# Two buffers for the raw attention outputs, one PSUM bank for the value products, three for the maximum scores

## The reference

```
xn = layernorm(x)
q, k, v = heads of (xn Wq^T / 4), (ctx Wk^T), (ctx Wv^T)
scores[q,k] = q.k + (q . p_params)[clip(q-k, -4, 4) + 4], -1e30 where k > q
x = x + tanh(g_xattn) * (softmax(scores) v, heads joined) Wo^T
```

## Time and profile before

| | us |
|---|---|
| median of 3 runs (lowest, highest) | 740.97 (736.86, 741.93) |
| the profiled execution: its time | 738.62 |
| its span | 736.7 |
| prologue, to the first score of unit 0 | 0 to 65.1 |
| units 0 to 5, start of each | 65.1, 103.2, 145.1, 185.5, 225.1, 265.6 |
| units 6 and 7, start of each | 306.0, 340.3 |
| end of the last value product of unit 7 | 369.7 |

### The profile page before, as it was taken

One profiled execution on the slowest core, in us unless ns is written; L12 is line 12 of the kernel. 1 busy time (PEld: TensorE's weight loads), 2 busy tenths in 40 slices (PEclk: granted clock), 3 DMA queues, 4 the chain that ended last, 5 costly groups with the idle time before them and its releaser, 6 DMA issues.

```text
span 736.7 us, 10646 instructions
## 1 busy us (share of the span) xinstructions
PE 628.5 (85%) x3384; PEld 484.8 (66%) x3384; DVE 460.5 (63%) x884; ACT 277.4 (38%) x501; POOL 176.7 (24%) x177
## 2 busy tenths in 40 slices
PE   3674968788878977888647999999999999999997
PEld 2553745457545754554325888888888888888886
DVE  3567657777578758762168475755747575665653
ACT  2432456244643465335333333323232333324222
POOL 2142004310341007100010223232323223232322
PEclk9756989899989999989868999999999999999999
DMA  7741133513344333454121103121211202121220
GB/s 234 210 103 36 30 86 85 114 41 86 72 107 97 73 78 95 99 168 127 40 48 60 57 7 98 41 87 57 81 63 53 91 1 100 43 86 58 74 72 28
DMA packets 39856, 58.65 MB, mean 80 GB/s; under 512 B 7984, under 2 KB 21040, under 8 KB 39792
## 3 DMA queue, kind: packets, MB, share of 16 engines
q1 hardware_dynamic: 39824, 58.25, 28.9%
HBM read 31.76 MB, written 4.85 MB: 50 GB/s over the span
## 4 chain that ended last, share of the span: by engine, by line
issue 49%; PE 20%; DVE 10%; POOL 8%; DMA 6%; SPq 3%; ACT 2%; POOLq 0%; DVEq 0%; ACTq 0%
POOL hl L1150 4%; PE oT L915 4%; PE smax L854 4%; SPq L277 2%; DMA qs<-mt 2%; DVE mx L582 2%; PE oT L919 2%; PE sT L895 2%; DMA at<-rden_d 2%; PE work L794 2%; PE sT L894 2%; DVE mx L609 1%; DMA rden_d<-dent 1%; POOL d L380 1%; PE work L825 1%
## 5 line engine op out<-in xcount | busy, mean ns | idle before, releaser
L1150 POOL TENSOR_TENSOR hl<-sg,hh 128x512 fp32r<-128x512 f32 x72 | 93.0, 1293 | 249.3 <-ACT hh L1193 249.3
L482 ACT ACTIVATE ex<-sT 128x512 f32<-128x512 f32 (+1 forms) x160 | 92.2, 590 | 152.1 <-PE sT L895 127.6
L1187 ACT ACTIVATE sg<-pg 128x512 f32<-128x512 f32 x72 | 43.0, 597 | 198.8 <-PE pu L1432 198.0
L854 PE MATMUL smax<-km,qs 96*128 96x308 f32 (+1 forms) x240 | 91.2, 412 | 27.1 <-DVE mx L582 19.3
L582 DVE TENSOR_REDUCE mx<-smax 128x2 f32<-128x308 f32 x184 | 82.9, 474 | 48.3 <-PE smax L854 45.4
L854 PEld LDWEIGHTS smax<-km,qs 96*128 96x128 f32 x240 | 47.8, 206 | 72.8 <-DVE mx L582 40.1
L1447 PE MATMUL py<-wxl,hh 128*128 128x256 f32 x288 | 81.8, 284 | 3.1 <-DVE x L1331 2.0
L1447 PE MATMUL py<-wxh,hl 128*128 128x256 f32 x288 | 80.9, 281 | 0.0
L1447 PE MATMUL py<-wxh,hh 128*128 128x256 f32 x288 | 80.6, 280 | 0.0
L1319 DVE TENSOR_TENSOR sg<-cwb,sg 128x512 f32<-128x512 f32 x64 | 67.2, 1050 | 11.3 <-DMA cwb<-cwt_d 8.4
L1314 DVE TENSOR_TENSOR sg<-pu,sg 128x512 f32<-128x512 f32 x72 | 49.2, 683 | 28.0 <-ACT sg L1187 26.6
(11 more groups left out here) (152 smaller groups left out, 1124.1 us busy)
## 6 DMA issues: line engine op xcount, KB each, us to landing
cwb<-cwt_d SPq DMA_DIRECT2D x64, 256.0 KB, 3.4
qs<-qh SPq DMA_DIRECT2D x64, 128.0 KB, 2.6
qs<-ql SPq DMA_DIRECT2D x32, 128.0 KB, 2.8
at<-rden_d SPq DMA_DIRECT2D x64, 64.0 KB, 2.2
out<-x SPq DMA_DIRECT2D x8, 512.0 KB, 4.4
ks<-km SPq DMA_DIRECT2D x16, 231.0 KB, 3.4
wx<-in_wx SPq DMA_DIRECT2D x9, 384.0 KB, 6.6
x<-in_x SPq DMA_DIRECT2D x3, 1024.0 KB, 8.8
```

What stands on the lines that cost most here:

```text
L482: nc.scalar.activation(ex[:, g % 2, i % 5, q0:HALF], ST[i % 2][:, q0:HALF], ACT.Exp).then_inc(exp_s, 1)
L854: last_one = nc.tensor.matmul(bank[:, k, 0:width], qs[0:96, s, tile * P:(tile + 1) * P], km[:, s, 0:width], start=True, stop=True)
L1150: nc.gpsimd.tensor_tensor(hl[:, i % R, :], sg[:, i % R, :], hh[:, i % R, :], ALU.subtract).then_inc(hl_done, 1)
L1187: nc.scalar.activation(sg[:, i % R, :], PG[i % RG][:], ACT.Silu).then_inc(sg_s, 1)
```

## The change

- `raws` is a pair: a new SBUF buffer `raw_first` for units with h=0 and the old `raw` for h=1. `raw_out` of unit u waits only for the division of unit u-2. `divisors` and `divide` take the buffer of their unit.
- `OT` is one bank. A value product of group g waits until the copy of the group before it is done. The copies move to after exponentials 9, 14, 19, and 4 of the next unit.
- `SM` has three banks, and block q = 2p + k uses bank q mod 3, so it waits for the reader of block q-3, where it was q-2. In the prologue the ring has five banks (three of `SM`, two of sT) in place of two pairs.

```diff
+    raw_first = sb("raw_first", [P, NG, HALF])
+    raws = (raw_first, raw)
...
-    SM = ctx.enter_context(nc.psum_tensor("smax", [P, 2, HALF], F32))
+    SM = ctx.enter_context(nc.psum_tensor("smax", [P, 3, HALF], F32))
...
-    M_START = (SM, STP)
-    OT = [ctx.enter_context(nc.psum_tensor(f"oT{i}", [P, HALF], F32)) for i in range(2)]
+    MAX_BANKS = [SM[:, i, :] for i in range(3)]
+    M_START = MAX_BANKS + ST
+    OT = ctx.enter_context(nc.psum_tensor("oT", [P, HALF], F32))
...
+    RING = 3
+    def is_near(h, q):
+        return h == 0 and m_tile(0, q // 2) < 2
+    def copied(q):
+        return sum(is_near(0, i) for i in range(q))
+    def reduced(h, q):
+        return sum(not is_near(h, i) for i in range(q))
...
-        def raw_out(u, g, start=False):
+        def raw_out(u, h, g):
             act.wait_ge(pv_ps, NG * u + g + 1)
-            if not start:
-                act.wait_ge(at_s, 2 * (u - 1) + g % 2 + 1)
-            nc.scalar.copy(raw[:, g, :], OT[g % 2][:]).then_inc(raw_s, 1)
+            if not (isinstance(u, int) and u < 2):
+                act.wait_ge(at_s, 2 * (u - 1))
+            nc.scalar.copy(raws[h][:, g, :], OT[:]).then_inc(raw_s, 1)
...
-                if i == 5 and carry:
-                    raw_out(u - 1, 3, start=(h == 1 and isinstance(b, int) and b == 0))
+                if i == 4 and carry:
+                    raw_out(u - 1, 1 - h, 3)
...
-                if i in (14, 17, 19):
-                    raw_out(u, (14, 17, 19).index(i), start=not carry)
+                if i in (9, 14, 19):
+                    raw_out(u, h, i // 5 - 1)
...
-                nc.vector.tensor_tensor(at[:, g, :], raw[:, g, :], at[:, g, :], ALU.mult).then_inc(at_s, 1)
+                nc.vector.tensor_tensor(at[:, g, :], raws[h][:, g, :], at[:, g, :], ALU.mult).then_inc(at_s, 1)
...
+            q = 2 * p + k
+            if q == 0:
+                pe.wait_ge(mx_s, 3 * NM * b + NM * h)
+            elif q >= RING and is_near(h, q - RING):
+                pe.wait_ge(sx_s, NM * b + copied(q - RING + 1))
+            elif q >= RING:
+                pe.wait_ge(mx_s, 3 * NM * b + NM * h + reduced(h, q - RING + 1))
+            stack_scores(m_tile(h, p), p, k, MAX_BANKS[q % RING])
...
-                if not (start and g < 2):
-                    pe.wait_ge(raw_s, NG * u + g - 1)
+                if not (start and g == 0):
+                    pe.wait_ge(raw_s, NG * u + g)
...
-                    nc.tensor.matmul(OT[g % 2][32 * j:32 * j + 32, :], va[:, 4 * g + j, :], ex[:, g % 2, j, :],
+                    nc.tensor.matmul(OT[32 * j:32 * j + 32, :], va[:, 4 * g + j, :], ex[:, g % 2, j, :],
```

More of the change, by code:

```diff
@@ L262, in m_stack, with divisors @@
                          mt[:, q0:HALF].unsqueeze(1).broadcast_to([32, NSTK, HALF - q0]).bitcast(F32)).then_inc(ms_in, 16)
-        def divisors(u):
+        def divisors(u, h):
+            kept = raws[h]
             sp.wait_ge(raw_s, NG * (u + 1))
-            sp.dma_start(den_d.rearrange("j (g n) -> j g n", g=NG), raw[HD::32, :, :]).then_inc(den_out, 16)
+            sp.dma_start(den_d.rearrange("j (g n) -> j g n", g=NG), kept[HD::32, :, :]).then_inc(den_out, 16)
             sp.wait_ge(den_out, 16 * (u + 1))
@@ L290, in unit @@
             if carry:
-                divisors(u - 1)
+                divisors(u - 1, 1 - h)
             if h == 1 and ahead:
@@ L324, in sync @@
         batches(sp, unit)
-        divisors(2 * B - 1)
+        divisors(2 * B - 1, 1)
     def gpsimd(pool):
@@ L460, in q_out, with near @@
                 nc.scalar.copy(qh[:, c, :], W[(use + c) % 2][:]).then_inc(q_hi, 1)
-        def near(b, p, bank=SM):
+        def near(b, p, banks=MAX_BANKS):
             for k in range(2):
-                act.wait_ge(sm_ps, 4 * NM * b + 2 * p + k + 1)
-                nc.scalar.copy(sx[:, m_tile(0, p), m_stacks(p).start + k, :], bank[:, k, 0:SW]).then_inc(sx_s, 1)
-        def raw_out(u, g, start=False):
+                q = 2 * p + k
+                act.wait_ge(sm_ps, 4 * NM * b + q + 1)
+                nc.scalar.copy(sx[:, m_tile(0, p), m_stacks(p).start + k, :], banks[q % len(banks)][:, 0:SW])\
+                    .then_inc(sx_s, 1)
+        def raw_out(u, h, g):
             act.wait_ge(pv_ps, NG * u + g + 1)
-            if not start:
-                act.wait_ge(at_s, 2 * (u - 1) + g % 2 + 1)
-            nc.scalar.copy(raw[:, g, :], OT[g % 2][:]).then_inc(raw_s, 1)
+            if not (isinstance(u, int) and u < 2):
+                act.wait_ge(at_s, 2 * (u - 1))
+            nc.scalar.copy(raws[h][:, g, :], OT[:]).then_inc(raw_s, 1)
         def unit(b, h, carry, ahead):
@@ L576, in k_lo, with maximum @@
                                                ALU.mult, ALU.subtract).then_inc(kl_s, 1)
-        def maximum(b, h, p, bank=SM):
+        def maximum(b, h, p, banks=MAX_BANKS):
             for k in range(2):
+                q = 2 * p + k
                 stk = m_stacks(p).start + k
-                dve.wait_ge(sm_ps, 2 * NM * (2 * b + h) + 2 * p + k + 1)
+                dve.wait_ge(sm_ps, 2 * NM * (2 * b + h) + q + 1)
                 nc.vector.reduce_max(mx[:, m_tile(h, p), 2 * stk:2 * stk + 2],
-                                     bank[:, k, 0:PAIR].rearrange("p (j k) -> p j k", j=2), AX_X).then_inc(mx_s, 1)
+                                     banks[q % len(banks)][:, 0:PAIR].rearrange("p (j k) -> p j k", j=2), AX_X)\
+                    .then_inc(mx_s, 1)
         def by_stack(ap):
@@ L642, in reciprocals, with divide @@
             nc.vector.reciprocal(dent[:], dent[:]).then_inc(rden_s, 1)
-        def divide(u, groups=range(2)):
+        def divide(u, h, groups=range(2)):
             dve.wait_ge(rden_in, 128 * (u + 1))
@@ L740, in vector @@
             if m_tile(0, p) >= 2:
-                maximum(0, 0, p, M_START[p % 2])
+                maximum(0, 0, p, M_START)
             if p == 8:
@@ L757, in last_residual @@
                 residual(B - 1, 1, pr, NW0 + Y_USE[0] + pr)
-        return lambda: reciprocals(2 * B - 1), lambda: divide(2 * B - 1), last_residual
+        return lambda: reciprocals(2 * B - 1), lambda: divide(2 * B - 1, 1), last_residual
     def tensor(pe):
@@ L978, in tensor @@
             for k in range(2):
[L980 to L988, removed]
+                q = 2 * p + k
+                last = q - len(M_START)
+                if last >= 0 and is_near(0, last):
+                    pe.wait_ge(sx_s, copied(last + 1))
+                elif last >= 0:
+                    pe.wait_ge(mx_s, reduced(0, last + 1))
+                stack_scores(m_tile(0, p), p, k, M_START[q % len(M_START)])
         max_T(0, 0, -1, START + 12)
```

28 lines of the change are left out of this document (8 added, 20 removed).

## The result

The changed kernel took 729.42 us (median of 4 runs, 728.44 to 732.39) beside 741.45 for the kernel before (4 runs, 736.86 to 742.01), a ratio of 0.9844 with a 95% interval of 0.9811 to 0.9876. It is 1.6% faster, 12.0 us by the medians, where 727 was forecast; the time stands inside the range of 719 to 735. The profiled execution took 729.36 us with a span of 727.3, against 738.62 and 736.7 before.

A forecast was written before the change was run, and what follows sets the result against it. PE carries most work, so its idle places at waits for maxima and a raw copy count. 5.3 + 7.2 + 0.4 + 0.5 = 13.4 us off 738.62 gives 725.2, or 727.6 from the median: forecast 727, range 719 to 735.

The forecast's parts named there:

- (a): Units 1, 3 and 5, step 16: the ring moves work into PE's pause, 2.4 us three times, 7.2 in all.
- Rival B: The clock is not lowered after the shorter pause at step 16, 3 x 2 us more: 721 us, chance 0.11.
- DVE behind POOL: Units 1, 3 and 5: two divisions still take 4.4 us beside POOL's 3.61 us subtraction; the pause can only be filled.
- The single bank: Value products: one bank costs nothing, as the copy ends 1.5 us early; 0.1 to 0.3 us a group in units 6, 7.
- Rival D: The copy is late at the single bank, 31 products lose 0.6 us each, 18.6 in all: 746 us, chance 0.06.
- (b): Unit 7: PE's 6.03 us wait for the raw copy goes and the projection starts 5.3 us earlier, a gain that stays.
- (c): Unit 6, step 15: one block moves ahead of PE's 2.52 us pause for maxima, 0.4 us gained.
- The prologue: Before unit 0: with five banks the fifth block no longer waits 0.77 us for a copy; 0.5 us, bounds 0 and 0.8.
- Units 2 and 4: PE's early pause there: no gain counted, since the transposes behind it need DVE's normalised rows, which come at the same time.
- (2): Units 1, 3, 5: value matmuls before a 2.5 to 2.9 us pause ending at DVE's maximum, clock about 0.5, 2.4 us shorter each.
- Rival C: The step 16 pause is not filled because the value product is held there; only 5.3 + 0.4 + 0.5 remain: 735, chance 0.09.
- E: Rival: unit 7 gives nothing because its end is held by its own division's DMA chain: 733 us, chance 0.08.

The follow-up runs named there:

- e2: The changed kernel with the ring of maximum scores back at two banks, four in the prologue: 737.75 us, ratio 0.9953 to the kernel before.
- e5: The changed kernel with the odd units' value product of step 16 put behind the second block of maximum scores: 735.92 us, ratio 0.9931 to the kernel before.
- e6: The changed kernel with POOL's subtraction done for half of the stacks only, so less work and different output: 720.25 us, ratio 0.9745 to the kernel before.
- e4: The changed kernel with DVE's divisions in the odd units moved behind the maxima of step 17: 724.16 us, ratio 0.9783 to the kernel before.
- e1: The kernel before with the second raw buffer alone, keeping its ring of two and two product banks: 739.16 us, ratio 0.9986.
- e9: The changed kernel with the odd units' divisions behind step 17 and two maximum banks again in even units: 723.07 us, ratio 0.9762 to the kernel before.
- e3: The changed kernel with four banks in the prologue instead of five, the ring of three kept inside the units: 731.37 us, ratio 0.9875 to the kernel before.
- b2: The kernel before, unchanged, profiled a third time: 739.53 us.
- b1: The kernel before, unchanged, profiled a second time: 745.28 us.
- e8: The changed kernel with divisions behind step 17 and ten unused matmuls ahead of unit 7's projection: 723.52 us, ratio 0.9784 to the kernel before.

## Why the prediction was right, and where its terms were not

**(a) Units 1, 3 and 5: right.** Forecast 7.2 us, measured 7.0 (2.9, 2.0 and 2.1). e2 takes the ring away and loses the whole gain of these units; e5 takes the filling alone away and loses 5.4. What failed is the length of the pause: "some 2.7 us" is the 3.89 less the moved 1.2, with PE's arrival left where it was. But with the ring PE also comes to step 16 earlier: score 16 starts 0.33 us after POOL's subtraction starts (283.88 and 283.55), where before it was 1.56 (288.07 and 286.51). So it waits those 1.2 us more, 3.87 in all. Since what sets the end of the pause is POOL's chain, an earlier arrival is no gain, and the 2.4 stood. Rival B (the clock stays high) lived on a shorter pause, which never came; e6 shows that at 2.16 us it would have held.

**DVE behind POOL: right.** In e6 1.71 us off POOL's operation are 1.71 us off DVE's two divisions, and in e4, outside it, they take 1.32. That is what the Trainium skill states (SBUF — State Buffer, Who interferes with whom): a DVE instruction with two SBUF inputs contends with a GpSimd instruction that reads SBUF. But the prediction's "the pause cannot vanish, only be filled" holds for this order of work alone: in e4 it vanished.

**The single bank: right.** Forecast nothing, measured 0.6 us in sum, and e2 is not slower than e1. Rival D, 18.6 us of waits, is refuted; other matmuls stand between two products, and these are the cover. It can be thin: the copy at 283.76 in unit 5 ends at 284.39, and the products that need the bank start at 284.45. The rule of the Trainium skill (Perfetto Trace Analysis, Matmuls) that independent groups should rotate through PSUM banks had nothing to give here.

**(b) Unit 7: mechanism right, the term of 5.3 us mis-sized.** The projection did start 5.3 us earlier (18.38 us after the unit's first score in place of 23.69), within 0.3 us of the division's end. The unit gained 3.6. The step that failed is "Unit 7's last products, its copy, and the experts' start hang behind it in one line, so the gain stays". They do hang behind it, but the row of 3.62 us for the projection was taken at the upper clock, and I let it stand. Before, the value matmuls and scores that stood between the 6 us pause and the projection ran at the lower clock, and the projection behind them at the upper. Now they stand ahead of the pause, and the projection itself comes first behind it: 5.41 us, 1.8 more. In the executions where the projection is fast, the unit's first products were slow and the division was 1.4 us later. Either way some 1.7 us of the 5.3 are given back. Nor are the 3.6 us assured: in the variants without a fill (e2 to e6 and e9) it took 26.70 to 28.44 us, and then the gain over 29.36 is 0.9 to 2.7: in e3 to e6 its first products and the projection were both slow, and in all but e6 DVE waited 8.8 to 9.1 us for the DMAs of the division, not 7.8. The second buffer without the ring is worth still less: in e1 the division started 18.64 us after the first score, after a wait of 9.06 for its DMAs, and the pause was 3.8.

**(c) Unit 6: too small.** Forecast 0.4, measured 1.5. The step that failed is that "the reciprocals stand at step 9 of DVE's order and were not waiting, so the DMA lands when it does now". Step 9 itself comes earlier, because the unit's first steps lost their small waits: the reciprocals start at 10.36 us after the first score in place of 11.36, first in the changed kernel, whose unit 6 starts at 300.73, then in the one before, at 305.98.

```profile
311.09 0.54 DVE L665 RECIPROCAL dent<-dent 128x64 f32<-128x64 f32 x1
...
319.04 0.69 DVE L671 TENSOR_TENSOR at<-raw,at 128x512 f32<-128x512 f32 x1 [3.55 <-DMA at<-rden_d]
...
320.18 0.62 PE L872 MATMUL smax<-km,qs 96*128 96x308 f32 x1 [4.09 <-DVE mx L604]
```

```profile
317.34 0.54 DVE L642 RECIPROCAL dent<-dent 128x64 f32<-128x64 f32 x1
```

The pause ends at 19.45 us where before it ended at 20.13 (326.11 less 305.98), which is 0.7 of the 1.0 us by which unit 6 is shorter in this pair (33.36 and 34.33); the rest may be the block moved ahead. PE arrives earlier still, so its pause here is 4.09 us, not 2.52.

**The prologue: in part chance, and otherwise open.** Forecast 0.5, measured 1.5 over three profiles each, and 3.2 in the first pair. b2 shows the kernel before with a start at 62.36, and e3 has the early start with four banks. The difference lies in which stretch runs at the lower clock. That this is chance alone is not shown: up to the start of unit 1 the six profiles with four banks in the prologue (before, b1, b2, e1, e2, e3) took 100.39 to 103.59 us, mean 102.1, and the eight with five 98.94 to 101.03, mean 100.2. In five of the six the lower clock fell on query projections or on the first value products of unit 0, in one of the eight it did. So the fifth bank may be worth more than its 0.5 us.

**Units 2 and 4: nothing was forecast, 0.8 us each were lost.** In the first pair it was 2.7 and 1.0; two more profiles of each kernel brought it down, and within one kernel unit 2 scatters by 2.0 us. The argument that the transposes wait for DVE's rows in any case held: in unit 2 they start 8.19 us after the first score, where before it was 8.20. What it left out is the clock. With the block moved ahead, PE stands idle for 1.68 and 0.63 us in front of them, where it was 1.45 and 0.24, and the value products behind run at the lower clock. Unit 2 of the changed kernel, and then the same products of the kernel before:

```profile
146.41 0.41 PE L872 MATMUL smax<-km,qs 96*128 96x308 f32 x1 [1.68 <-DVE mx L604]
147.44 0.66 PE L806 MATMUL work<-idr,xn 128*128 128x128 f32 x4 [0.63 <-DVE xn L560]
...
148.52 1.63 PE L933 MATMUL oT<-ex,va 128*32 128x512 f32 x8
```

```profile
154.40 1.06 PE L915 MATMUL oT<-ex,va 128*32 128x512 f32 x8
```

These products were slow (1.6 to 1.9 us) in units 2 and 4 of all three profiles of the changed kernel, and of the three before in b1's alone. Unit 4 takes 41.4 to 42.7 us in every profile in which they are slow, and 40.2 to 40.5 in every other, e4, e6 and e8 among them, which have the ring. What brings the lower clock there is open: in e9 the pause was 1.46 and 1.45 us again and the products were slow all the same, and the moved copy of group 3 was not tried alone.

Of the signs named ahead, (1), (3), (4) and (5) came as written. (2) came in the place of the products, the clock and the releaser, but the pause is 3.87 us. The units' gain lies between 2.0 and 2.9. Rival C is refuted by the rows of unit 5, E by unit 7's 3.6 us.

## What to carry to other kernels

Where an engine must wait for another whose end is fixed by a third, look for work of its own that stands behind the pause and can be put ahead of it: 2 us a unit came from that, and from removing the other engine's waits alone nothing that could be told. When a pause moves, ask what will stand behind it: it may run at the lower clock, so price it by a row taken at that clock too. And before a difference of 1 or 2 us between two profiles gets an explanation, profile the kernel before a second and third time.

## What was not expected of the hardware

- Which stretch runs at the lower clock differs between executions of one program. In the kernel before the query projections of the prologue took 0.63 us a matmul in one execution and 0.39 in another, and unit 0 started at 65.11 or 62.36.
- After a pause of 2.16 us the granted clock was 1.00, after 3.87 it was 0.50. The length of the pause alone did not decide: a shorter one of 1.84 us left the projection at 3.72 us, and one of 1.92 came before a projection of 5.41.
- A store of the 32 KB of reciprocals takes 1.5 us to its semaphore in most units, 1.9 in unit 7, and now and then 2.6 to 3.2 (2.67 in b2's unit 2, 3.0 in unit 7 of e3, 3.2 in unit 7 of e5). It does not set the division's time alone: in unit 7 DVE waited 8.98 us for the division's DMAs in e3, and 9.03 in e2 with a store of 1.9.
